# GpSimd's share of a weighted sum: half loads in six slots in turn, six steps of t instead of four, and the bias from TensorE

## What is computed

```python
h = jax.nn.sigmoid(jnp.einsum('bts,st->bs', x, W1) + b1)   # x: B x T x S, W1: S x T
y = h @ W2.T + b2                                          # W2: S x S
```

## Time and profile before

| | |
|---|---|
| runs | 321.3 us median of 3 (320.53 to 323.89) |
| the profiled execution | 322.97 us, its span 321.2 us |
| busy: PE, DVE, POOL, ACT | 269.7, 261.1, 166.0, 45.0 us |
| read from HBM | 105.48 MB |
| mean granted clock of TensorE | 0.963 |

### The profile page before, as it was taken

How to read it: one execution, slowest core, us unless ns; L and a number is a source line. 1 busy time by engine, 2 the same in 40 slices (tenths; PEclk the granted TensorE clock), 3 DMA queues, 4 the chain that set the end, 5 groups by cost and what they waited for, 6 DMA issues and landing times.

```text
span 321.2 us, 4852 instructions
## 1 busy us (share of the span) xinstructions
PE 269.7 (84%) x1825; PEld 231.9 (72%) x1825; DVE 261.1 (81%) x392; ACT 45.0 (14%) x79; POOL 166.0 (52%) x63
## 2 busy tenths in 40 slices
PE   0846868648889999999799999949999988599775
PEld 0746767548768888888588888848888967488664
DVE  0717999929999988889998888988888999377956
ACT  1201212002262001000500000040111140000030
POOL 0009687600009999942399750059889419760000
PEclk9969989969999999999999999998999999799999
DMA  7999999999999999999999999999999996996006
GB/s 237 407 388 390 386 385 386 400 386 387 385 386 384 369 386 387 386 387 376 371 312 375 384 384 389 383 375 373 373 372 373 361 348 217 349 294 203 1 0 261
DMA packets 67367, 109.99 MB, mean 342 GB/s; under 512 B 3208, under 2 KB 40080, under 8 KB 67344
## 3 DMA queue, kind: packets, MB, share of 16 engines
q1 hardware_dynamic: 66608, 107.06, 93.7%
q10 hardware_dynamic: 736, 2.63, 2.0%
HBM read 105.48 MB, written 4.19 MB: 341 GB/s over the span
## 4 chain that ended last, share of the span: by engine, by line
PE 60%; DMA 27%; SPq 4%; issue 4%; DVE 4%; DVEq 0%
PE xbank L206 31%; DMA ring<-in_r_x 27%; PE pbank L263 24%; PE xbank L291 3%; DVE acc L315 2%; SPq L175 2%; SPq L169 2%; PE pbank L235 1%; PE pbank L291 1%; DVE w_lo L322 1%; DVE acc L312 0%; DVE y L330 0%; SPq L177 0%; SPq L157 0%; DVE h_lo L348 0%
## 5 line engine op out<-in xcount | busy, mean ns | idle before, releaser
L315 DVE SCALAR_TENSOR_TENSOR acc<-xbank,w,acc 128x512 f32<-128x512 f32 x304 | 215.6, 745 | 45.1 <-PE xbank L206 43.5
L206 PE MATMUL xbank<-ident,ring 128*128 128x128 f32 x1280 | 189.4, 284 | 40.9 <-DMA ring<-in_r_x 39.4
L206 PEld LDWEIGHTS xbank<-ident,ring 128*128 128x128 f32 x1280 | 157.4, 146 | 72.7 <-issue 25.2
L437 POOL TENSOR_TENSOR nat<-nat,w1all 128x2048 f32<-128x2048 f32 (+2 forms) x15 | 55.5, 3703 | 13.7 <-DMA nat<-in_r_x 13.7
L440 POOL TENSOR_TENSOR nsum<-nsum,nat 128x2048 f32<-128x2048 f32 (+2 forms) x15 | 55.5, 3702 | 1.2
L445 POOL TENSOR_TENSOR h_lo<-h,h_hi 128x512 fp32r<-128x512 f32 x14 | 17.5, 1279 | 74.3 <-ACT h_hi L410 74.3
L263 PE MATMUL pbank<-w_hi,h_hi 128*128 128x512 f32 x112 | 49.7, 444 | 0.0
L263 PE MATMUL pbank<-w_lo,h_hi 128*128 128x512 f32 x112 | 48.1, 429 | 0.0
L263 PE MATMUL pbank<-w_hi,h_lo 128*128 128x512 f32 x112 | 41.9, 439 | 0.0
L435 POOL TENSOR_TENSOR nsum<-nat,w1all 128x2048 f32<-128x2048 f32 (+2 forms) x5 | 18.5, 3697 | 22.0 <-ACT w1all L363 22.0
L381 ACT ACTIVATE h<-acc,b1col 128x512 f32<-128x512 f32 (+1 forms) x22 | 11.6, 597 | 107.3 <-DVE acc L315 107.3
(11 more groups left out here) (33 smaller groups left out, 86.9 us busy)
## 6 DMA issues: line engine op xcount, KB each, us to landing
ring<-in_r_x SPq DMA_DIRECT2D x40, 1024.0 KB, 14.3
ring<-in_r_x SPq DMA_DIRECT2D x40, 768.0 KB, 11.8
ring<-in_r_x SPq DMA_DIRECT2D x20, 512.0 KB, 8.2
nat<-in_r_x SPq DMA_DIRECT2D x8, 1024.0 KB, 14.3
nat<-in_r_x SPq DMA_DIRECT2D x8, 768.0 KB, 11.0
y<-in_L_rec_W SPq DMA_DIRECT2D x2, 2048.0 KB, 14.8
out_y<-y ACTq DMA_DIRECT2D x4, 512.0 KB, 6.4
nat<-in_r_x SPq DMA_DIRECT2D x4, 512.0 KB, 8.4
```

What stands on the lines that cost most here:

```text
L206: mm = pe.transpose(xbank[u % XBANKS][:, j * P:(j + 1) * P], tile[:, j, :], ident[:, :])
L315: nc.vector.scalar_tensor_tensor(out=acc[:, c, rows], in0=xbank[u % XBANKS][:, rows], scalar=weight, in1=acc[:, c, rows], op0=ALU.mult, op ...
L437: nc.gpsimd.tensor_tensor(slot, slot, row, ALU.mult).then_inc(nat_weighed, 1)
```

## The change

POOL takes 4 t of stage 0 and 6 of each later one. Each is loaded in two halves (two row tiles each, *parts*: 512, 384 or 256 KB) into six half slots in turn, `nsum` is gone: a part, once multiplied in its slot, gets the part two before it added in that slot, and PE turns the last two slots. The places run ahead: two parts of the next stage stand at the end of each. POOL makes `h_lo` of stage i - 1 after the third part of stage i. `ring` has five slots. b2 is no longer loaded to all partitions: its rounded and its low part lie in two rows of `b2x`, zeros elsewhere, and one matmul with `ones` opens each kept sum. ACT makes `h` and `h_hi` chunk by chunk, and the product waits for single chunks; its first two output tiles take all their high parts first. The lead is 2 units per chunk, and in the last stage the product is due by three fifths of the units.

```diff
-NK = 4
 STAGES = (
-    (0, 4, 0, 4, (2, 4, 10, 14), "keep"),
-    (0, 4, 4, 4, (0, 3, 10, 14), "last"),
-    (4, 4, 0, 3, (0, 3, 10, 14), "keep"),
-    (4, 4, 3, 3, (0, 3, 10, 14), "add"),
-    (4, 4, 6, 2, (0, 3, 10, 14), "last"),
+    (0, 0, 4, 4, (2, 3, 5, 7, 9, 11, 13, 15, 17, 18), "keep"),
+    (0, 4, 4, 6, (0, 2, 3, 5, 6, 8, 9, 11, 12, 14, 15, 17), "last"),
+    (4, 0, 3, 6, (0, 2, 3, 5, 6, 8, 9, 11, 12, 14, 15, 17), "keep"),
+    (4, 3, 3, 6, (0, 2, 3, 5, 6, 8, 9, 11, 12, 14, 15, 17), "add"),
+    (4, 6, 2, 6, (0, 2, 3, 5, 6, 8, 9, 11, 12, 13), "last"),
 )
-    RING = 6
-    NATS = 2
+    RING = 5
+    NATS = 6
...
-        nat = sb("nat", [P, NATS, JT, BANK])
-        nsum = sb("nsum", [P, JT, BANK])
+        nat = sb("nat", [P, NATS, HALF, BANK])
-        b2all = sb("b2all", [P, O])
+        b2x = sb("b2x", [P, O], F32R)
+        ones = sb("ones", [P, P], F32R)
...
+            return 3 * chunks[i] + (fate[i] == "keep")
-            steps = outs[i - 1] * 3 * chunks[i - 1]
-            lead = 10 * JT // tiles[i]
-            span = (len(units[i]) * 4) // 5 - lead
+            steps = OUTS * steps_of(i - 1)
+            lead = 2 * chunks[i]
+            span = len(units[i]) * (4 if i < LAST else 3) // 5 - lead
             return max(0, min(steps, -(-(v - lead + 1) * steps // span)))
...
+                for at in range(T - pools[i]):
                     if at in places:
-                        if m >= NATS:
-                            sp.wait_ge(nat_freed, m - NATS + 1)
+                        s, k, f = parts[m]
+                        if m >= NATS and parts[m - NATS][1] < pools[parts[m - NATS][0]] - 1:
+                            sp.wait_ge(nat_added, sums_made(m - NATS + 2))
+                        elif m >= NATS:
+                            sp.wait_ge(unit_turned, sum_turned(parts[m - NATS][0]))
...
-                    if i == 0 and at == 17:
+                    if i == 0 and at == 13:
                         sp.wait_ge(w2_turned, SC)
...
+                high = 2 * nch + bias
+                if k < 2 * high:
+                    n, r = divmod(k, high)
+                elif k < 2 * per:
+                    n, r = (k - 2 * high) // nch, high + (k - 2 * high) % nch
...
+                if r < bias:
+                    pe.matmul(pbank[n % 2][:, :], ones[:, :], b2x[:, cols], start=True, stop=False)
...
                     if i < LAST:
-                        sigmoid(i, c, slice(0, wide[i]))
+                        sigmoid(i, c, slice(0, BANK))
+                        act.wait_ge(h_ready, first_h[i] + c + 1)
+                        nc.scalar.copy(h_hi[:, c, :], h[:, c, :]).then_inc(h_hi_ready, 1)
...
+            for m, (i, k, f) in enumerate(parts):
+                weigh(m)
+                if k > 0:
+                    add_sum(m)
+                if i > 0 and k == 1 and f == 0:
+                    low_parts(i - 1)
```

More of the change, by code:

```diff
@@ L36, in rec_kernel @@
     CMAX = 4
-    RING = 6
-    NATS = 2
+    RING = 5
+    NATS = 6
     XBANKS = 6
     assert (B, T, S, O) == (2 * BANK, 24, 1024, 1024)
-    tiles = [s[1] for s in STAGES]
-    chunks = [s[3] for s in STAGES]
-    wide = [n * P for n in tiles]
+    chunks = [s[2] for s in STAGES]
+    pools = [s[3] for s in STAGES]
     fate = [s[5] for s in STAGES]
+    NK0, NK = pools[0], max(pools)
+    HALF = JT // 2
     units = []
[L49 to L52, removed]
+    for i in range(NS):
+        order = [("x", t, c) for t in range(pools[i], T - 2) for c in range(chunks[i])]
+        order += [("n", 0, c) for c in range(chunks[i])]
+        order += [("x", t, c) for t in range(T - 2, T) for c in range(chunks[i])]
         units.append(order)
@@ L56, in rec_kernel, with sum_turned, sums_made @@
     first_h = [sum(chunks[:i]) for i in range(NS)]
[L58 to L61, removed]
+    OUTS = OH * JT
+    kept_at = [OUTS * sum(f == "keep" for f in fate[:i]) for i in range(NS)]
+    added_at = [OUTS * sum(f != "keep" for f in fate[:i]) for i in range(NS)]
     item_of, item_end = {}, []
     for i in range(NS):
-        for t in range(NK, T):
+        for t in range(pools[i], T):
             item_of[i, t] = len(item_end)
             item_end.append(first_unit[i] + units[i].index(("x", t, chunks[i] - 1)))
+    parts = [(i, k, f) for i in range(NS) for k in range(pools[i]) for f in range(2)]
+    first_part = [2 * sum(pools[:i]) for i in range(NS)]
+    def sum_turned(i):
+        return first_unit[i] + units[i].index(("n", 0, chunks[i] - 1)) + 1
+    def sums_made(m):
+        return m + 1 - 2 * (parts[m][0] + 1)
     def chunk_end(i, c):
-        return first_unit[i] + max(v for v, (_, _, cc) in enumerate(units[i]) if cc == c) + 1
+        return first_unit[i] + max(v for v, u in enumerate(units[i]) if u[2] == c) + 1
     x_v = x.rearrange("(j p) t s -> p j t s", p=P)
@@ L195, in turn_unit @@
                     pe.wait_ge(unit_added, u + 1 - XBANKS)
[L196 to L206, removed]
+                end = first_part[i] + 2 * pools[i]
+                if kind == "x" and c == 0:
+                    pe.wait_ge(x_loaded[item_of[i, t] % RING], 16 * (item_of[i, t] // RING + 1))
+                elif kind == "n" and c == 0:
+                    pe.wait_ge(nat_added, sums_made(end - 1))
+                for j in range(JT):
+                    if kind == "x":
+                        tile = ring[:, item_of[i, t] % RING, j, c * P:(c + 1) * P]
+                    else:
+                        tile = nat[:, (end - 2 + j // HALF) % NATS, j % HALF, c * P:(c + 1) * P]
+                    mm = pe.transpose(xbank[u % XBANKS][:, j * P:(j + 1) * P], tile, ident[:, :])
                 mm.then_inc(unit_turned, 1)
             def turn_set(q):
-                half, k = divmod(q - 1, NK)
-                if q == 1 + NK:
+                if q == EARLY:
                     pe.wait_ge(w_lo_ready, SC)
@@ new lines, in weigh @@
+            def weigh(m):
+                i, k, f = parts[m]
+                _, c0, n, _, _, _ = STAGES[i]
+                row = w1all[:, k, c0 * P:(c0 + n) * P].unsqueeze(1).to_broadcast([P, HALF, n * P])
+                slot = nat[:, m % NATS, :, :n * P]
+                pool.wait_ge(nat_loaded[m % NATS], 16 * (m // NATS + 1))
+                if k == 0 and f == 0 and i < 3:
+                    pool.wait_ge(set_kept, (EARLY, EARLY + NK, SETN)[i])
+                nc.gpsimd.tensor_tensor(slot, slot, row, ALU.mult).then_inc(nat_weighed, 1)
@@ L442, in low_parts, with add_sum @@
+            def add_sum(m):
+                i, k, _ = parts[m]
+                n = STAGES[i][2]
+                slot = nat[:, m % NATS, :, :n * P]
+                pool.wait_ge(nat_weighed, m + 1)
+                if k > 1:
+                    pool.wait_ge(nat_added, sums_made(m - 2))
+                nc.gpsimd.tensor_tensor(slot, slot, nat[:, (m - 2) % NATS, :, :n * P], ALU.add).then_inc(nat_added, 1)
             def low_parts(i):
```

222 lines of the change are left out of this document (104 added, 118 removed).

## The result

| | before | after | forecast |
|---|---|---|---|
| median of 20 runs each | 321.37 us | 319.19 us (317.51 to 320.92) | 311.0 |
| the profiled execution and its span | 322.97, 321.2 | 320.03, 318.2 | 312.7, 310.9 |
| mean granted clock of TensorE | 0.963 | 0.949 | |

What follows compares the result with a forecast made beforehand. Transfers with holes from SP's waits for POOL bound it, then PE in the last stage: 259.8 + 18 x 1.35 + 11.1 + 15.7 = 310.9 us of span, 311.0 as the median; range 305 to 319.

Steps and rivals of the forecast that it cites:

- third item of the last stage: Third ring load of the last stage, there at 259.8 us: 262.9 before, less b2 (1.4) and earlier holes (1.7).
- 18 units with steps: Last stage, after its third ring load: 72 product steps, four on each unit at 1.35 us, ending at 284.1 us.
- 15 units to chunk 0's end: Last stage, after the product's steps: 10.1 us of units plus 1.0 for an add and the pipe, to 295.2 us.
- chunk 0's end to the span's: The kernel's end: sigmoids, 24 x 2 matmuls, sums and stores, left alone by the change at 15.7 us.
- The holes and their maker: Transfer gaps from SP waiting 27.7 us for POOL; halves fill them: 0.3 + 1.4 us before stage 4, 6.7 in it.
- PE is the later of the two in the last stage: After the third ring load PE, not the transfers, sets the end; x can be in 4 to 6 us sooner.
- rival 3: PE isn't the last: DVE and PE catch up sooner and transfers set the end, 305.4 us; 12%.
- rival 2: The halved loads' size costs transfer rate, 6.6 us more: 317.6 us; 10%.
- rival 4: Five ring slots are too few: 1 to 2 us lost at four boundaries, a cold clock behind each, 316 us; 8%.
- rival 5: POOL becomes the bound, 18 operations in a row behind each `h_lo`; with 0.7 us more each, 336 us; 5%.
- 24 units fewer: Two t more for POOL in four stages: 16 us less work for DVE, 11 us less for PE.
- Rival 6: The holes only move: PE holds the ring, the last stage takes its 43 us as before, 318.5 us; 5%.

Runs made afterwards that it cites:

- a_warm_tail: The changed kernel with 14 unused matmuls in PE's idle time ahead of the end's matmuls: 317.37 us, ratio 0.989.
- b_place: The kernel before with POOL's last two loads of the last stage at places 12 and 15 instead of 10 and 14: 320.51 us, ratio 0.998.
- a_warm_few: The changed kernel with the last product due by four fifths, 11 unused matmuls at the last stage's start and 13 before the end: 314.29 us, ratio 0.974.
- a_45_tail: The changed kernel with the last product due by four fifths and 14 unused matmuls before the end: 315.54 us, ratio 0.977.
- a_pool4_ring6: The changed kernel with 4 t for POOL in all stages and six ring slots instead of five: 319.39 us, ratio 0.989.
- a_pool4: The changed kernel with 4 t for POOL in all stages, halves and five ring slots kept: 319.39 us, ratio 0.990.
- a_last_4_5: The changed kernel with the last stage's waiting product laid up to four fifths of its units instead of three fifths: 317.38 us, ratio 0.987.

## Why the prediction was wrong

The step that failed is "from there to the span's end stand 15.7 us of sigmoids, 24 x 2 matmuls, sums and stores, which the change leaves alone". The change touches none of these instructions, but they took 19.3 us in the profiled execution. 2.8 of the 3.6 us more are the clock's: 14 of the 48 matmuls ran at 1.2 GHz, and with a_warm_tail, which keeps the clock up, the time is gone. The other 0.8 are the last wait for a store, which goes with six t for POOL. The number 15.7 was read from an end that happened to be at full clock. The 3.6 us are half of the 7.3 by which the span was off; the rest is in two other terms of the sum, the third item (2.0) and the units with steps (1.9). The Trainium skill's "TensorE: Matmul & The Clock Gate", under "What's actually happening", says that the throttled clock is the default and activity lifts it; the prediction should have asked what activity is left. Its remark there that the ramp costs under 1% of a typical kernel's span is no guide here, where the clock falls again later: 2.8 us in the end and 1.2 at the last stage's start are 1.3% of 318, more than the change won.

Point by point, with the profiled execution (forecast 310.9 us of span, measured 318.2):

| step | said | measured | |
|---|---|---|---|
| third item of the last stage | 259.8 | 261.8 | +2.0 |
| from there, 18 units with steps | 24.3 | 26.2 | +1.9 |
| 15 units to chunk 0's end | 11.1 | 10.9 | -0.2 |
| chunk 0's end to the span's | 15.7 | 19.3 | +3.6 |

- *The holes and their maker*: right in the main. They went, and b_place shows that where the one wait of the last stage stands in SP's order is worth 5.0 us at chunk 0's end. But the sum of SP's waits for POOL was 42.6 us, not 27.7, and it was not the sum that made the holes: b_place has 41.9 us of such waits and no hole in the last stage.
- *The third item*: 2 us off. It came 1.1 us sooner than before instead of 3.1. The bytes ahead of it were loaded about as worked out: at 256 us 0.45 MB more had been moved than before, with 0.52 of b2 fewer to move, 0.97 MB or 2.6 us. Its last byte's turn had come by 258.1 us, but it landed 3.6 us behind that, where before it was 2.0; with 2.0 it would have been in at 260.1. Why a load trails the bytes ahead of it by more when halves stand among them isn't settled; the sixth slot, tried with 4 t, didn't mend it (262.7).
- *Steps at full clock* (18 x 1.35): 1.9 us short. The first unit with steps took 265.09 - 262.53 = 2.56 us for 1.35, at a clock of 0.72 and 0.85; PE had idled 2.13 us for the third item. The other 0.7 is spread over the units. The clock's part can be had back: a_warm_few took 33.8 us from the third item to chunk 0's end, a_45_tail without its eleven matmuls 35.4.
- *PE is the later of the two in the last stage*: right; x could have been in sooner (rival 3 needed PE to keep up, and it did not).
- *Halved loads cost no rate* (rival 2): right. 386, 373 and 348 before are 386, 373 and 345 now, with loads of 512, 384 and 256 KB among the others. So the rate goes with the row length and not with the size of the loads, at least where halves carry 23 of 100.7 MB. The Trainium skill's rule of at least 1 MiB, in "DMA: Bandwidth & Descriptors" under "Rules for kernel authors", is not borne out in this queue, which is always full.
- *Ring of five costs nothing* (rival 4): right by a_pool4_ring6 for 4 t; with 6 t it wasn't tried. Rival 4 named a cold clock behind the boundaries too, and one of the two cold places is there: the last stage's start, where PE had waited 2.13 us. The other, in the end, no rival had.
- *POOL isn't the bound* (against rival 5): right. A half takes 2.39 us (128x1024), 1.84 (128x768, said 1.85) and 1.28 (128x512); POOL is busy for 215 us, said 205. The last sum is made at 286.06 + 1.29 = 287.35 and turned at 292.52, and PE never waits for one. POOL's last sum, in order of time:

```profile
286.06 1.29 POOL L485 TENSOR_TENSOR nat<-nat 128x512 f32<-128x512 f32 x1
```
- *24 units fewer*: DVE is 13.3 us less busy (said 16), and that is worth nothing, which the prediction left open by not giving it a term. PE waits for ring loads (35.2 us by the page's groups) and DVE for PE, so the busy time saved becomes idle time; 4 t in place of 6 cost 0.2 us in the median, and with the product late and the end filled they were 0.7 us faster.
- *Rival 6* gave 318.5, close to the measured time, for another reason: it had the last stage take its 43 us as before. That stage became 5.5 us shorter (37.1 from the third item to chunk 0's end, 42.6 before), and the end longer.

What fixes whether the end is cold is open. Steps ending 7.7 us ahead left it warm before, 7.6 and 6.9 us ahead left it cold in b_place and with the product due by four fifths, and in a_pool4 it started warm 13 us behind them. Each of these is one profiled execution. The single runs speak for an end that falls either way from run to run. Of b_place's ten, the five with a mean granted clock of 0.968 took 319.5 to 320.1 us and the five with 0.950 to 0.957 took 320.9 to 321.4, the profiled one among them. Of the change's twenty, the two with the highest clock (0.973 and 0.978) took 317.5 and 317.6, the five with the lowest (0.949) 318.9 to 320.9, and the profiled one is again of the lowest. The kernels with unused matmuls spread over 0.2 to 1.1 us in four runs or three. But the mean over a run doesn't say where the clock was low, so this isn't shown.

## What to carry to other kernels

A tail that a change "leaves alone" keeps its length only if TensorE reaches it at the same clock, so read its granted clock before its old length goes into a sum, and add the cold case as a second value: PE's work ahead of it didn't tell here which of the two would come. If a dependent tail follows an idle stretch, fill the stretch with matmuls nobody reads, few enough to end before the real ones are ready. And when holes in the transfers have one maker, move that one load first: two numbers in a table and fourteen unused matmuls did about as much as a rewritten share, ring and order.

## What was not expected of the hardware

- A matmul of 128x512 takes 0.43 us at the low clock and 0.23 at the high one, and in the end 14 in a row ran at the low one (5.7 us) before it rose, though PE was busy throughout.
- Transposes without a gap for 4.0 us (b_place) and 3.6 us (a_last_4_5), or nearly so for 8.5 us (the change), and then 3.4 to 3.7 us of idleness were followed by the low clock; 4.0 us of them and 3.7 us of idleness were followed by the high one before.
- The filled kernels seem steadier too: 317.20 to 317.66 us in four runs with fourteen unused matmuls, against 317.51 to 320.92 in twenty without. The one run of 526.6 us (a_45_tail) stands against it.
- The last wait for a store is 1.7 us in seven profiles with 4 t for POOL and 2.5 us in six with 6 t.
- Seventeen unused matmuls at the start of a stage gave no more than none, eleven gave 1.3 us: with seventeen the first turn behind them began at 263.4 us, with eleven at 262.2.
